# A sandwich transformer layer on eight cores: tiles of x normalized at once, transposed one tile ahead, and half of the last denominators moved

## The reference

```python
def attn(x, w_q, w_k, w_v, w_o):            # D = S = 2048, 16 heads of 128
    q, k, v = x @ w_q.T, x @ w_k.T, x @ w_v.T        # by heads
    p = softmax(q @ k.T / sqrt(128))
    return (p @ v) @ w_o.T
def ffn(x, w_gate, w_up, w_down):           # hidden 8192
    return (silu(x @ w_gate.T) * (x @ w_up.T)) @ w_down.T
x = x + layernorm(attn(layernorm(x)))       # eps 1e-5, no weights
x = x + layernorm(ffn(layernorm(x)))
```

## Time and profile before

| | us |
|---|---|
| median of three runs (2303.87 to 2578.17) | 2305.51 |
| the profiled execution | 2302.86 |
| its slowest core, core 3, first to last instruction | 2301.0 |
| PE busy on that core | 2253.4 (98%) |
| DVE busy, ACT busy, POOL busy | 574.2, 584.1, 132.9 |
| PE idle that ends with DVE writing `xn` (14 times) | 31.3 |
| PE idle that ends with ACT writing `ln3t` (once) | 3.4 |
| PE idle that ends with ACT writing `kt` (15 times) | 3.3 |

### The profile page before, as it was taken

The page is one execution under the profiler, slowest core; times in us unless marked ns, Lnnn a source line. Parts: engine busy times, 40 slices in busy tenths (PEclk is TensorE's granted clock), DMA queues, the critical chain, the costliest instruction groups (busy, mean ns, idle before and its releaser), DMA issues.

```text
span 2301.0 us, 26963 instructions; the slowest of 8 cores (2297.2 to 2301.0 us)
## 1 busy us (share of the span) xinstructions
PE 2253.4 (98%) x10656; PEld 1025.6 (45%) x10656; DVE 574.2 (25%) x771; ACT 584.1 (25%) x774; POOL 132.9 (6%) x252
## 2 busy tenths in 40 slices
PE   4999999999999999999999999999999999999998
PEld 2444444444444444444444444444444444444443
DVE  6500044554554556610000110000110000000005
ACT  3411166666666653410000000000000000000003
POOL 0000000000000000000000000000000010000000
PEclk9999999999999999999999999999999999999999
DMA  9521011411414153454444444444444474434447
GB/s 258 143 41 26 8 30 28 74 25 31 65 28 74 28 110 144 116 89 75 81 74 75 81 74 75 81 74 74 81 75 74 73 137 73 80 67 83 72 84 256
DMA packets 45051, 186.33 MB, mean 81 GB/s; under 512 B 4992, under 2 KB 4992, under 8 KB 39808
## 3 DMA queue, kind: packets, MB, share of 16 engines
q0 software_dynamic: 36864, 134.27, 35.1%
q1 hardware_dynamic: 8064, 50.34, 6.2%
HBM read 302.06 MB, written 16.78 MB: 139 GB/s over the span
## 4 chain that ended last, share of the span: by engine, by line
PE 94%; ACT 2%; issue 2%; DMA 1%; DVE 1%; SPq 0%; DVEq 0%; ACTq 0%
PE ps L165 94%; DMA xs<-xb 1%; DVE xn L238 1%; ACT ln1t L171 0%; ACT kt L171 0%; ACT pt L168 0%; ACT pvc L171 0%; ACT sdv L168 0%; DVE st L583 0%; DVE st L230 0%; SPq L162 0%; DVE sdv L222 0%; ACT tt L168 0%; ACT x L168 0%; DVEq L159 0%
## 5 line engine op out<-in xcount | busy, mean ns | idle before, releaser
L165 PE MATMUL ps<-ln3t,we 128*128 128x512 bf16 x4000 | 864.3, 379 | 0.0
L165 PEld LDWEIGHTS ps<-ln3t,we 128*128 128x128 bf16 x4000 | 391.2, 98 | 470.8
L165 PE MATMUL ps<-ln1t,w 128*128 128x512 bf16 x1536 | 371.7, 379 | 3.3 <-ACT kt L171 3.3
L168 ACT ACTIVATE pt<-ps,kon 128x1024 bf16<-128x1024 f32 x256 | 285.2, 1115 | 190.4 <-PE ps L165 190.4
L168 ACT ACTIVATE sil<-ps 128x512 f32<-128x512 f32 x128 | 76.4, 597 | 778.5 <-PE ps L165 778.5
L165 PEld LDWEIGHTS ps<-ln1t,w 128*128 128x128 bf16 x1536 | 147.9, 97 | 190.2 <-issue 15.5
L165 PE MATMUL ps<-wvs,ln1t 128*128 128x512 bf16 x1024 | 227.4, 383 | 0.0
L165 PE MATMUL ps<-ring,ga 128*128 128x512 bf16 x1024 | 222.1, 379 | 0.4
L165 PE MATMUL ps<-ring,gb 128*128 128x512 bf16 x1024 | 221.8, 379 | 0.0
L165 PEld LDWEIGHTS ps<-ring,ga 128*128 128x128 bf16 x1024 | 100.0, 98 | 121.9 <-issue 1.8
L165 PEld LDWEIGHTS ps<-ring,gb 128*128 128x128 bf16 x1024 | 100.2, 98 | 121.0 <-issue 0.5
(11 more groups left out here) (56 smaller groups left out, 892.3 us busy)
## 6 DMA issues: line engine op xcount, KB each, us to landing
ring<-wd POOLq DMA_DIRECT2D x64, 512.0 KB, 6.2
we<-wu POOLq DMA_DIRECT2D x63, 512.0 KB, 6.1
we<-wg POOLq DMA_DIRECT2D x62, 512.0 KB, 6.1
xs<-xb SPq DMA_DIRECT2D x16, 1024.0 KB, 11.1
wvs<-wv POOLq DMA_DIRECT2D x16, 512.0 KB, 11.7
w<-wq POOLq DMA_DIRECT2D x16, 512.0 KB, 6.4
w<-wk POOLq DMA_DIRECT2D x16, 512.0 KB, 6.1
xr<-xb SPq DMA_DIRECT2D x8, 1024.0 KB, 5.9
```

The costliest lines, as they stand in the source:

```text
L165: return op("t", lambda e: e.matmul(dst, lhsT, rhs, start=start, stop=stop), ctr)
L168: return op("s", lambda e: e.activation(dst, src, fn, bias=bias, scale=scale), ctr)
```

## The change

Tiles 0 to 5 go through a new function, `x_at_once`, which takes the statistics and the norm of the same tile and then issues the next load. T(5) moves behind the last parts of V(0) to V(3), and from V(4) on the transposes run one tile ahead: T(k+1), then V(k), with the root of tile k+1 called ahead of T(k+1) and so ahead of its evictions. The second half of the last head's denominators moves from behind piece 3's first 15 matmuls to behind piece 9 and `o_norm(1)`. One new root of a constant on ScalarE follows the last `pvc` copy.

```diff
--- before.py
+++ after.py
@@ -312,28 +312,33 @@
     for tc in range(5):
         x_load(tc)
     wv_load(0, [x_in[tc] for tc in range(4)])
-    x_stats(0)
+
+    def x_at_once(tc):
+        x_stats(tc)
+        x_norm(tc)
+        x_load(tc + 5)
+
 
     for tc in range(4):
-        x_norm_behind(tc + 1)
+        x_at_once(tc)
         x_transpose(tc)
         if tc:
             for t in range(tc):
                 v_part(t, 0, tc - 1)
             for c in range(tc):
                 v_part(tc, 0, c)
-    for tc in (4, 5):
-        x_norm_behind(tc + 1)
-        x_transpose(tc)
-        for t in (2 * tc - 8, 2 * tc - 7):
-            v_part(t, 0, 3)
-            v_out(t, 0)
-    x_norm_behind(7)
+    x_at_once(4)
+    x_transpose(4)
+    x_at_once(5)
+    for t in range(4):
+        v_part(t, 0, 3)
+        v_out(t, 0)
+    x_stats(6)
     for k in range(4, NTC):
-        if k + 2 < NTC:
-            x_transpose(k + 2)
-        if k + 4 <= NTC:
-            x_norm_behind(k + 4)
+        if 5 <= k and k + 2 <= NTC:
+            x_norm_behind(k + 2)
+        if k + 1 < NTC:
+            x_transpose(k + 1)
         v_proj(k, 0)
     wv_load(1, [x_in[tc] for tc in (7, 9, 11, 13)])
     wt("g", x_in[NTC - 1])
@@ -549,12 +554,13 @@
     pv(H - 1, 14)
     oproj(1, 14)
     pv(H - 1, 15)
-    for n in (2, 3):
+    op("s", lambda e: e.activation(KON.r(2, 1), EPSC, AF.Sqrt))
+    for kc in range(15):
+        oproj(2, kc)
+    denominators(H - 1, 0, 0)
+    for n in (3, 4):
         for kc in range(15):
             oproj(n, kc)
-        denominators(H - 1, n - 2, n - 2)
-    for kc in range(15):
-        oproj(4, kc)
 
     dXR = [C("dXR%d" % i) for i in range(3)]
     dXS = [C("dXS%d" % i) for i in range(3)]
@@ -672,6 +678,8 @@
         o_stats(n)
         if j == 1:
             o_norm(qc - 1)
+        if n == 9:
+            denominators(H - 1, 1, 1)
         if j == 3:
             o_chain(qc)
     for m in range(3, 9):
```

## The result

The changed kernel takes 2330.36 us (median; 2328.52 to 2330.46) against 2304.77 for the kernel before, run beside it. The ratio is 1.0113 [1.0101, 1.0126]: 26.3 us more, a change that is smaller than the 2% named above, but clear of the noise of these runs. The forecast was 2332 in 2318 to 2344. The profiled execution took 2328.52; its slowest core, core 6, spans 2326.8 and the shortest, core 2, 2323.0. Before it was 2301.0 on core 3.

A forecast was written before the change was run, and what follows sets the result against it. The prediction took PE, busy 98% of the span, as the bound, so only its pauses and clock matter. It summed 2302.86 + 17.3 (pauses) + 10.5 (clock) + 1.7 (moved denominators) to 2332 us, range 2318 to 2344.

The forecast's parts named there:

- Step 2: Opening, transposes one tile ahead: ten pauses of 2.95 us ahead of T(6) to T(15), 7.46 a tile; cost 17.3 us.
- Step 1: Opening, tiles 0 to 5 at once: landings of `wvs` unchanged, T(4) at about 39.4 us, T(5) at 44.2.
- Step 3: Opening: 10/16 of the ten pauses followed by half clock at 1.68 us each; cost 10.5 us, bounds 0 and 29.
- Step 4: Output projection: t3(0,1) waits 5.2 us for the moved reciprocal, t3(0,3) no longer waits; cost 1.7 us, 0 to 2.7.
- Rival 1: Opening: all ten pauses fall to half clock, 16.8 us for the clock, 2339 in all; chance 0.13.
- rival 2: Opening: all ten pauses fall at the dear price, 29 us for the clock, 2351 in all; chance 0.05.
- rival 3: Opening: the clock holds at all ten pauses, 0 us for the clock, 2322 in all; chance 0.06.
- Rival 4: Opening: root not held by the eviction of V(k), pauses stay 0.26 us, T(15) at 91.9, 2295 in all; chance 0.05.
- Rival 5: Opening: "roots ahead of evictions" holds for the transposes, not the projection; part of the forecast, no size or chance.

The follow-up runs named there:

- e3: Changed kernel with the eviction of V(k) called behind the statistics and root of the next tile; ratio to the kernel before 1.0007, undisturbed runs 2298.35 to 2300.16 us.
- e9: Changed kernel unedited, run again on the experiments' chip; 2345.41 us, ratio 1.0154 to the kernel before.
- e2: Changed kernel with the denominators put back where they were; 2329.36 us, ratio 1.0126 to the kernel before.
- e5: Changed kernel with the root of tile k+3 called ahead of T(k+1); ratio to the kernel before 1.0013, undisturbed runs 0.9963.
- e6: Kernel before with the moved denominators copied out of bank 1 by ScalarE, reciprocal taken from the copy in four pieces; undisturbed 2298.92 us, ratio 0.9978.
- e1: Kernel before with only the moved denominators and the root of a constant; ratio 1.0117, run again (e1_again) 1.0127.
- e4: Changed kernel with 12 extra unused matmuls ahead of each of T(6) to T(15); ratio to the kernel before 1.0157, undisturbed run 2323.55 us.
- e7: Edits of e5 and e6 together in one kernel; undisturbed 2289.59 us against 2304.06 for the kernel before, ratio 0.9938.
- e8: Kernel before with the moved denominators and 22 extra unused matmuls ahead of t3(0,1); ratio 1.0026, undisturbed runs 2303.37 to 2303.98 us.

## Why the prediction was right

The sum was 2332 and the kernel took 2330.36, and the mechanisms of the sum are the ones in the rows. Two terms were too dear, by 2.2 and 3.8 us.

- **Step 2, the ten pauses: right.** 2.92 us was measured for the 2.95 taken, 7.43 a tile for 7.46, each pause ended by `xn`, the root 0.50 behind the eviction into `vt`. e3 shows the cause by moving that one entry alone.
- **Step 1, T(5) and T(6): a landing wrong.** "I take their landings as unchanged" failed. Piece 2 of `wvs`, issued at 17.81, landed in 14.2 us instead of 16.1, and the matmuls on it start at 32.11 instead of 34.2, so T(4) comes at 37.28 instead of 39.4. Piece 3 landed at 23.48 + 15.0 = 38.5 instead of 40.4; its parts end 3.45 later, at 42.02, and T(5) follows at 42.05. The chain of root and norm behind T(4) is as the step had it, 2.1 earlier at each point: the root at 39.69, the norm at 40.45, and T(5) 1.60 after that. PE's parts and the norm now come together, within 0.03. T(6) is at 49.48 instead of 51.7: the step was 2.2 us too dear. Why the landings were shorter was not tried.
- **Step 3, the clock: the price right, the count wrong.** A fall cost 1.68 (5.30 - 3.62), as taken (only the first on core 6 cost 2.9). But "the share of the rows", 10 of 16, is not what ten pauses in a row give: four fell on core 3, at every third and at the last, so 6.7 us for the 10.5. The share mixed first pauses with second ones, which on six cores came 5.7 to 5.8 us after the first; here a pause comes every 7.43. That the distance makes the difference is not shown: on cores 1 and 2 the second pause came 7.4 and 7.1 after the first, and half clock followed it too. The Trainium skill (TensorE: Matmul & The Clock Gate, Part 1, "HAM oscillation — how this bites in real kernels") tells of a fall at every one of a kernel's waits, of about 3 to 5 us each; taken over to these ten pauses it gives 16.8. The traces disagree with that here, with four falls at ten pauses of 2.92.
- **Step 4, the moved denominators: right.** 4.99 us for the 5.2, ended by `rec`; none ahead of t3(0,3); half clock behind it. On core 3 the place lost 7.21 instead of 5.17, so +2.0 where 1.7 was forecast in 0 to 2.7; e9 against e2 gives 2.3 to 2.5.

The balance on core 3: T(15) at 121.81, its 0.89, 32 matmuls of 0.216 and one more fall of 1.7 give 131.3 for the end of V(15), 22.0 after the 109.3 of before. With 2.0 from step 4 that is 24.0, and the span grew by 23.8. The slowest core is another one now, core 6, whose span is 2.0 longer than core 3's; that makes up the rest of the 25.7 between the profiled executions. So it is in part luck that the forecast lay as near as it did: these 2.0 us, of which it said nothing, and the 1.8 from the profiled execution to the median stand against the 6.0 that were too dear.

Rival 1 (all ten fall), rival 2 (all dear) and rival 3 (the clock holds) fell with the four falls. Rival 4 fell too, since the root was held each time; what it would have brought, e3 built by the order of the calls: T(15) at 94.82 on core 5, where the rival had 91.9. Rival 5 holds: the roots are ahead of the evictions of transposes and behind those of the projection.

## What to carry to other kernels

In an engine that takes its list in order, ask of each small step on a critical path which entry stands ahead of it and what that entry waits for: here a root of 0.28 us behind an eviction that waits for PE cost 2.92 us a tile, and either a place one entry earlier (e3) or work for one tile later (e5) took it away. When the distance between a producer and its consumer is cut from two tiles to one, count what is left in the bottleneck's list while the whole chain goes by. A PSUM bank should be emptied by the quickest copy there is, and the slow operation done from the copy, when it would stand in a busy engine's list (e6).

## What was not expected of the hardware

After the 5.0 us pause at t3(0,1), which ends on all eight cores between 886.8 and 889.8 us of their own spans in e1_again, some pairs of cores run on at a granted clock of 0.81, between the two levels. Stretches of e1_again, core 4, and then of its core 3:

```profile
897.00:1000.00 103.00, 102.11 (x458) 46.49 (x467) 53.20 (x95) 32.45 (x59) 3.18 (x6) 0.81 0.40 114
1000.00:1050.00 50.00, 49.65 (x200) 21.39 (x203) 4.13 (x6) 5.65 (x10) 2.65 (x5) 0.81 0.32 57
...
897.00:1000.00 103.00, 103.00 (x565) 50.26 (x564) 54.67 (x99) 36.53 (x66) 3.19 (x6) 1.00 0.44 123
```

Cores 4 and 5 ran so for about 160 us and came out some 26 us longer (2329.5 and 2330.2 against 2301.5 to 2304.9); the other six were at 1.00. Of the runs that enter the ratios, those of kernels with this pause held such a pair, or more cores, in 5 of 5 of e1, 3 of 9 of e3, 3 of 4 of e4, 3 of 6 of e5 and 2 of 4 of e9, together 16 of 28, and in none of 4 of the changed kernel on the first chip. Without the pause it was 2 of 36 of the kernel before, 1 of 4 of e2 and none of 12 of e6 and e7, together 3 of 52; with the pause filled (e8) 2 of 7. So on this chip it is likelier with the pause than without; whether filling the pause makes it rarer is not shown by so few runs. What triggers it, and on which pair, stays open. The Trainium skill (TensorE: Matmul & The Clock Gate, Part 1) tells of a limiter that takes a whole die to 13/16 of the clock once three of its cores run dense matmuls, for as long as the load lasts. The traces kept here don't agree: all eight cores run dense matmuls at 1.00 nearly throughout, and where 0.81 came it was on two cores of a die of four and ended while they went on.
